# Graph network layer: 49 edge groups for 50, dense units inside stage A, source indices loaded first, and gathers paced one by one

## The reference

```python
def _L0_gnn_ref(x, edge_index, W1, b1, W2, b2):
    x_col = x[col]
    feat = jnp.concatenate([x_col, x[row] - x_col], axis=-1)
    h = jax.nn.relu(feat @ W1 + b1)
    messages = h @ W2 + b2
    out = jax.ops.segment_max(messages, col, num_segments=x.shape[0])
    return jnp.where(jnp.isneginf(out), jnp.zeros_like(out), out)
...
def _L1_gnn_ref(x, edge_index, W1, b1, W2, b2, Wres, bres):
    agg = jax.ops.segment_sum(x[src], dst, num_segments=x.shape[0])
    h = x + agg
    h = jnp.maximum(h @ W1 + b1, 0.0) @ W2 + b2
    return x @ Wres + bres + h
...
x = _layernorm(x + _L0_gnn_ref(x, edge_index, ...), axis=-1)
x = _layernorm(x + _L1_gnn_ref(x, edge_index, ...), axis=-1)
```

## Time and profile before

| what | value |
|---|---|
| median of 3 timed executions | 1454.56 us (1453.96 to 1475.86) |
| the profiled execution: its own time | 1442.36 us |
| its span, from first to last instruction | 1440.5 us |
| PE busy over the span | 1176.8 us (82%) |
| DVE, ACT, POOL busy | 1085.9, 818.3, 833.3 us |
| mean granted clock of PE | 0.957 of full speed |
| moved by DMA | 236.11 MB, 164 GB/s on the mean |

### The profile page before, as it was taken

How to read it: one execution, slowest core, us unless ns; L and a number is a source line. 1 busy time by engine, 2 the same in 40 slices (tenths; PEclk the granted TensorE clock), 3 DMA queues, 4 the chain that set the end, 5 groups by cost and what they waited for, 6 DMA issues and landing times. The chain is left out here.

```text
span 1440.5 us, 32925 instructions
## 1 busy us (share of the span) xinstructions
PE 1176.8 (82%) x7573; PEld 862.2 (60%) x7573; DVE 1085.9 (75%) x5525; ACT 818.3 (57%) x2320; POOL 833.3 (58%) x812
## 2 busy tenths in 40 slices
PE   3899999972277777777669998999899999999992
PEld 1667777651133334334357877887776777777771
DVE  6698999862177777777748897897787888888881
ACT  1355555541155555555426665665657777777772
POOL 2666666666666666665066666666655555555513
PEclk9899999987599999999879999999999999999996
DMA  3666666643256655556445565655655555556541
GB/s 96 179 193 195 204 199 196 194 130 94 53 175 175 171 176 168 169 172 156 122 123 177 173 194 160 193 182 165 177 177 152 175 180 184 182 188 187 180 142 50
DMA packets 162414, 236.11 MB, mean 164 GB/s; under 512 B 27296, under 2 KB 70526, under 8 KB 162369
## 3 DMA queue, kind: packets, MB, share of 16 engines
q1 hardware_dynamic: 135184, 195.53, 42.8%
q0 software_dynamic: 25600, 39.60, 11.3%
q10 hardware_dynamic: 1584, 0.53, 0.1%
HBM read 131.05 MB, written 90.91 MB: 154 GB/s over the span
## 5 line engine op out<-in xcount | busy, mean ns | idle before, releaser
L576 POOL DMA_INDIRECT out<-edge_rows,idx x200 | 201.7, 1008 | 190.7 <-issue 127.7
L1221 PE MATMUL psY<-wcr,xT 128*128 128x128 f32 x1568 | 305.3, 276 | 0.0
L1220 PE MATMUL psY<-wc,hT 128*128 128x128 f32 x1568 | 304.8, 276 | 0.5 <-issue 0.5
L569 POOL DMA_INDIRECT edge_rows<-x1e_table,idx x200 | 206.1, 1031 | 151.2 <-issue 96.9
L569 POOL DMA_INDIRECT edge_rows<-in_x,idx x200 | 214.0, 1070 | 134.4 <-issue 64.8
L569 POOL DMA_INDIRECT xd_rows<-in_x,idx x200 | 209.2, 1046 | 120.6 <-issue 63.9
L1220 PEld LDWEIGHTS psY<-wc,hT 128*128 128x128 f32 x1568 | 256.2, 194 | 7.3 <-issue 0.8
L1072 ACT ACTIVATE o_rows<-psY,rs_b 128x128 f32<-128x128 f32 x784 | 223.6, 368 | 56.0 <-issue 40.3
L1221 PEld LDWEIGHTS psY<-wcr,xT 128*128 128x128 f32 x1568 | 240.0, 193 | 0.0
L1231 PE MATMUL psH<-xT,wc 128*128 128x512 f32 x392 | 212.9, 625 | 16.7 <-issue 9.7
L1052 ACT ACTIVATE sd_a<-mv_a,eps_col 128x4 f32<-128x4 f32 x196 | 58.4, 298 | 274.4 <-issue 150.5
(11 more groups left out here) (131 smaller groups left out, 2132.2 us busy)
## 6 DMA issues: line engine op xcount, KB each, us to landing
x_in<-in_x SPq DMA_DIRECT2D x196, 256.0 KB
out<-o_rows SPq DMA_DIRECT2D x196, 256.0 KB
xs_rows<-edge_rows SPq DMA_DIRECT2D x100, 256.0 KB
xs_rows<-src_dram SPq DMA_DIRECT2D x50, 256.0 KB
mask<-mask_dram SPq DMA_DIRECT2D x100, 128.0 KB
x1e_table<-shared SPq DMA_DIRECT2D x50, 256.0 KB
x1eT_spill<-x1eT SPq DMA_DIRECT2D x50, 256.0 KB
x1eT<-x1eT_spill SPq DMA_DIRECT2D x50, 256.0 KB
```

The source lines that it names most:

```text
L569: nc.gpsimd.indirect_dma_start(to, None, table, bass.IndirectOffsetOnAxis(idx[:, what, t:t + 1], 0), bounds_check=rows - 1, oob_is_err=err ...
L576: nc.gpsimd.indirect_dma_start(table, bass.IndirectOffsetOnAxis(idx[:, SCAT, t:t + 1], 0), frm, None, bounds_check=N - 1, oob_is_err=False ...
L1220: t_.matmul(to[:, cut(t)], h[:, cut(t)], wc2[:, :], start=False, stop=False, skip_group_check=True)
L1221: last = t_.matmul(to[:, cut(t)], xt[:, cut(t)], wcr[:, :], start=False, stop=t == TILES - 1, skip_group_check=True)
```

## The change

- GROUPS becomes 49 (the number of groups that hold an edge), with one quad that holds a single group at the end.
- Stage A is walked in octets of eight steps, and ahead of every even step stands one dense unit: six octets take bodies 14 to 19. Stage B has bodies 20 to 31, and stage C begins with body 32 and keeps 17 of its 23 bodies.
- The source indices are loaded ahead of x, on a semaphore of their own, cast and transposed at once (SRC_IDX_STEP, step 2 of DVE's setup), and POOL begins its source gathers after that step.
- POOL's source groups 38 to 48 are gathered one by one behind destination groups 4, 8, 12, ... 44.
- `pace` and `issued_pair` give way to `one_behind`: every transfer signals `s_issued`, and POOL issues one when all but the latest have signalled.
- The counter of a scatter's group is loaded ahead of the last transfer of the group before.

```diff
-    GROUPS = 2 * -(-E // (2 * ROWS))
...
+    GROUPS = -(-E // ROWS)
...
+    OCTETS = GROUPS // (2 * SLOTS)
+    FIRST_A = 1 + QUADS
+    FIRST_B = FIRST_A + OCTETS
     FIRST_C = FIRST_B + QUADS - 1
+    SRC_FIRST = GROUPS - 11
...
-            def quad_a(j):
-                for r in range(SLOTS):
-                    step_a(j, r)
+            def octet_a(i, b):
+                for r in range(2 * SLOTS):
+                    j = i * 2 + r // SLOTS
+                    if r % 2 == 0:
+                        dense(b, r // 2)
+                    step_a(j, r % SLOTS)
...
+            sp.wait_ge(s_iz, 1)
+            load_indices(0, src, s_is)
             for k in range(3):
                 load(0, k)
...
-            pool.wait_ge(s_dv, IDX_STEP)
+            pool.wait_ge(s_dv, SRC_IDX_STEP)
...
-            def pace(kw):
+            def one_behind():
+
+                wait(pool, s_issued, issued[0] - 1)
                 issued[0] += 1
-                if issued[0] % 2 == 0:
-                    kw["engine_sem"] = s_issued
-
-            def issued_pair():
-                if issued[0] % 2 == 0:
-                    pool.wait_ge(s_issued, issued[0] // 2)
...
-            for g in range(GROUPS):
+            for g in range(SRC_FIRST):
                 gather_src(g)
                 if g == GROUPS // 2:
+                    pool.wait_ge(s_dv, IDX_STEP)
                     for d in range(SLOTS):
                         gather_dst(d)
+            late = SRC_FIRST
             for g in range(SLOTS, GROUPS):
                 gather_dst(g)
+                if g % 4 == 0 and late < GROUPS:
+                    gather_src(late)
+                    late += 1
...
+            def stores_needed(g):
+                earlier = pool.value_load(stores_16[0:1, g:g + 1], min_val=0, max_val=16 * LAST)
+                return pool.snap(earlier + 16)
...
                 for t in range(TILES):
+                    if t == TILES - 1 and g + 1 < WHOLE:
+                        count = stores_needed(g + 1)
                     scatter(out, edge_rows[:, cut(g * TILES + t)], g * TILES + t, final[r])
...
+            dve.wait_ge(s_is, 16 * 3)
+            link(v.tensor_copy(idx_f[:, 0, :, :], idx_in[:, 0, :, :]))
             norm1_stats(0, 0)
             norm1_ready(0, 0)
             norm1_var(0, 0)
+            dve.wait_ge(s_pe, 1)
+            link(v.tensor_copy(idx[:, 0, :], psE[0][:, 0:2 * P]))
```

More of the change, by code:

```diff
@@ L50, in gnn_program @@
     assert UNITS == BODIES * SLOTS and N % 32 == 0
-    GROUPS = 2 * -(-E // (2 * ROWS))
-    PAIRS = GROUPS // 2
+    GROUPS = -(-E // ROWS)
+    OF_PARITY = [len(range(q, GROUPS, 2)) for q in range(2)]
     ETILES = GROUPS * TILES
@@ L325, in walk @@
             quad_s(0, 1)
-            with eng.Fori(1, QUADS - 1) as j:
+            with eng.Fori(1, QUADS - 2) as j:
                 quad_s(j, j + 1)
-            quad_s(QUADS - 1, QUADS)
+            for j in (QUADS - 2, QUADS - 1):
+                quad_s(j, j + 1)
             lead_a()
[L330 to L334, removed]
+            octet_a(0, FIRST_A)
+            with eng.Fori(1, OCTETS - 1) as i:
+                octet_a(i, i + FIRST_A)
+            octet_a(OCTETS - 1, OCTETS - 1 + FIRST_A)
+            for r in range(SLOTS):
+                step_a(QUADS - 1, r)
             lead_b()
             quad_b(0, FIRST_B)
-            with eng.Fori(1, QUADS - 1) as j:
+            with eng.Fori(1, QUADS - 2) as j:
                 quad_b(j, j + FIRST_B)
+            quad_b(QUADS - 2, QUADS - 2 + FIRST_B)
             quad_b(QUADS - 1, None)
@@ L496, in step_b, with load_indices @@
                 feed_b(j, r + 1)
+            HALF = P * P
+            def load_indices(n, a, done):
+                sp.dma_start(idx_in[:, n, 0, :], a[0:HALF].rearrange("(j p) -> j p", p=P)).then_inc(done, 16)
+                sp.dma_start(idx_in[0:FULL - P, n, 1, :],
+                             a[HALF:FULL * P].rearrange("(j p) -> j p", p=P)).then_inc(done, 16)
+                sp.dma_start(idx_in[FULL - P:FULL - P + 1, n, 1, 0:REST],
+                             a[FULL * P:E].rearrange("(j p) -> j p", j=1)).then_inc(done, 16)
+            sp.wait_ge(s_iz, 1)
+            load_indices(0, src, s_is)
             for k in range(3):
                 load(0, k)
[L501 to L508, removed]
+            sp.wait_ge(s_iz, 2)
+            for n in (1, 2):
+                load_indices(n, dst, s_i)
             sp.dma_start(idx_in[:, 3, 0, :], dst[1:HALF + 1].rearrange("(j p) -> j p", p=P)).then_inc(s_i, 16)
@@ L539, in _ @@
         def _(pool):
-            nc.gpsimd.memset(idx_in[:, 0:2, :, :], 0)
+            nc.gpsimd.memset(idx_in[:, 0, :, :], 0).then_inc(s_iz, 1)
+            nc.gpsimd.memset(ident[:, :], 0.0)
+            nc.gpsimd.memset(center[:, :], -1.0 / P).then_inc(s_c2, 1)
+            nc.gpsimd.memset(idx_in[:, 1, :, :], 0)
             nc.gpsimd.memset(idx_in[:, 2, :, :], BIG)
             nc.gpsimd.memset(idx_in[:, 3:5, :, :], -1).then_inc(s_iz, 1)
-            nc.gpsimd.memset(ident[:, :], 0.0)
-            nc.gpsimd.memset(center[:, :], -1.0 / P).then_inc(s_c2, 1)
             pool.wait_ge(s_c2, 1)
@@ L948, in _ @@
             norm1_var(0, 0)
+            dve.wait_ge(s_pe, 1)
+            link(v.tensor_copy(idx[:, 0, :], psE[0][:, 0:2 * P]))
+            assert step[0] == SRC_IDX_STEP
             norm1_stats(0, 1)
@@ L1191, in _ @@
             pe.wait_ge(s_c, 1)
+            pe.wait_ge(s_dv, 1)
+            for h in range(2):
+                last = t_.transpose(psE[0][:, cut(h)], idx_f[:, 0, h, :], ident[:, :])
+            last.then_inc(s_pe, 1)
             pe.wait_ge(s_w, 16 * 11)
-            pe.wait_ge(s_dv, 1)
+            pe.wait_ge(s_dv, SRC_IDX_STEP + 1)
             t_.matmul(psE[2][:, 0:P], center[:, :], raw[:, W1R, :], start=True, stop=True)
@@ L1201, in _ @@
             pe.wait_ge(s_dv, SCAT_STEP)
-            for n in range(3):
+            for n in range(2):
                 for h in range(2):
-                    at = 2 * n + h
-                    last = t_.transpose(psE[at // 4][:, cut(at % 4)], idx_f[:, n, h, :], ident[:, :])
+                    last = t_.transpose(psE[1][:, cut(2 * n + h)], idx_f[:, 1 + n, h, :], ident[:, :])
             last.then_inc(s_pe, 1)
```

44 lines of the change are left out of this document (20 added, 24 removed).

## The result

| what | us |
|---|---|
| the changed kernel, median of 4 (1877.88 to 1888.19) | 1881.37 |
| the kernel before beside it, median of 4 (1453.96 to 1475.86) | 1460.53 |
| ratio, with its 95% interval | 1.2907 [1.2817, 1.2997] |
| span of its profiled execution, granted clock | 1880.2, 0.835 |

The forecast was 1371 us. The changed kernel took 29% longer than the kernel before, against 5.7% less.

What follows compares the result with a forecast made beforehand. No engine was full throughout: PE bound search, B and tail, a ring stage A. Terms -84 +14 -6.6 -4 -1.5 -1 -0.5 = -83.6 us gave span about 1357, time 1359, scaled by 1.0085 to 1371 us; range 1330 to 1420 us.

Steps and rivals of the forecast that it cites:

- Pacing: POOL's transfers: signalling each and waiting for all but the latest, starts come 1.31 us apart (bounds 1.31 and 1.57).
- Rival four: Stage A: POOL becomes the bound if dense work on DVE slows its gathers; 1495 us, chance 0.04.
- the 24 ns: What dense work costs a POOL gather: means 1070 ns mostly beside it, 1046 ns mostly without it.
- rival two: POOL's pace stays 1.57 us a transfer, so its last scatters end late: 39 us on top, 1410 us; chance 0.14.
- Does the stall go?: Start of stage A: the 51.5 us stall on late destination rows goes, as POOL's gathers end at 232 or 276 us.
- They enter stage A: One dense unit ahead of every even step: 16.9 us a pair, 24 pairs 406 us, +14 us with the stall gone.
- 84 off, 72 on: 24 dense units leave stage C, 84 us off at 3.49 us each, and add 72 us of work to stage A.
- the ring: Stage A's step: DVE, ACT and PE wait on each other in turn; even step about 10.0 us, odd 6.9.
- Tail: End of kernel: four scatters after the last store instead of eight, last starting 3.9 us on, not 10.6; -6.6 us.
- the slack: POOL's margin at the end: its chain ends at 1284 us, the last store lands at 1343; 59 us.
- slower: Outcome outside the 2% that can't be told from no change, on the slow side: chance 0.04.

Runs made afterwards that it cites:

- g_after: The changed kernel with no further edit, in a set where the kernel before took 1414.57 us: 1345.95 us, ratio 0.9511.
- h_no_dense_in_a: The changed kernel without dense units in stage A (bodies back in stage C), new pacing kept; kernel before 1414.5 us: 1316.56 us, ratio 0.9311.
- h_pairs: The changed kernel with the kernel before's pauses by pairs put back, all else kept; kernel before 1414.5 us: 1409.95 us, ratio 0.997.

## Why the prediction was wrong, step by step

**The step that failed is "Pacing".** Its claim on POOL held in part: the pause is gone and the gap is 0.30 us, but on the first kind starts are about 1.3 us apart in stage B and 1.50 in the search. It failed in what it left out. I priced the pause of 0.81 us on POOL alone, between bounds of 1.31 and 1.57 us a transfer, and never asked what it did for the other engines. On the second kind it is what lets them run: 29 to 33% of the time hang on it. Rival four was near in form (dense work and POOL's issuing hold each other up) but had the direction wrong for the second kind: it let DVE slow POOL, and here POOL slows all the others. On the first kind its direction shows in one stage. POOL of g_after in the search:

```profile
150.94 1.01 POOL L580 DMA_INDIRECT edge_rows<-in_x,idx  x1 [0.30 <-DMA edge_rows<-in_x,idx]
152.25 1.06 POOL L580 DMA_INDIRECT edge_rows<-in_x,idx  x1 [0.31 <-DMA edge_rows<-in_x,idx]
153.62 1.56 POOL L580 DMA_INDIRECT edge_rows<-in_x,idx  x1 [0.30 <-DMA edge_rows<-in_x,idx]
```

And POOL's busy time over 170 us, with the number of transfers, first of g_after, then of the changed kernel on the second kind:

```profile
60.00:230.00 170.00, 134.31 (x113) 1.00 0.74 217
```

```profile
60.00:230.00 170.00, 121.84 (x122) 0.51 0.22 59
```

Where PE and DVE run the search, a transfer takes 1.19 us on the mean (35 of the 113 over 1.3 us) and starts are 1.50 us apart; in the same stage with the others mostly standing still, 1.00 us and 1.39. So the 24 ns, read from a kernel with pauses, were too small, and 1.31 us was too short for the search; PE didn't have to wait for these gathers. Dense work alone isn't what lengthens them: in stage B, with PE at 98%, a transfer takes 1.02 us (the third of the windows below, 244.86 us for 241). What in the search does it is not shown, nor whether it has to do with the starving. Nothing in the rows of before could give the size, as in them no third transfer ever stands right behind two others. That was in the text, as an argument for rival two. It should have been the argument for a case on the slower side.

The Trainium skill, page "SBUF — State Buffer", section "Who interferes with whom", says that DMA never contends with a compute engine, and that only a port pair shared by DVE and GpSimd does. The 16 to 20% of PE in these runs are no proof against it, since the path is not known, but PE, which by that section shares no port with GpSimd, stood still as much as DVE. Whoever reads the rule as "gathers can't slow PE" is wrong by nearly a factor of five here (95% against 20%, one kernel on the two kinds).

**The rest can be judged on the first kind,** where the forecast of 0.9426 (1371/1454.56) met 0.9511. The windows of g_after: search, stage A, stage B, stage C.

```profile
28.00:285.00 257.00, 245.48 (x2006) 189.57 (x2034) 237.89 (x1239) 150.30 (x429) 181.57 (x155) 0.99 0.69 206
288.00:729.00 441.00, 328.22 (x1555) 201.45 (x1576) 308.50 (x1381) 243.66 (x615) 231.36 (x224) 0.96 0.53 156
755.00:1076.00 321.00, 314.64 (x2159) 261.92 (x2184) 281.82 (x1411) 210.77 (x657) 244.86 (x241) 0.99 0.61 190
1100.00:1318.00 218.00, 214.85 (x1449) 171.04 (x1465) 189.62 (x1190) 170.45 (x508) 125.64 (x119) 1.00 0.56 181
```

*Does the stall go?* Right. PE starts on xd_rows at 288.5 us and runs to the last step without a gap of tens of us.

*They enter stage A.* Too small. From 288.5 to 729.0 us are 24 pairs, 18.35 us each, inside the bounds of 13.5 to 18.9, but 1.45 above the 16.9 taken: 35 us in all. The same stage without them, in h_no_dense_in_a:

```profile
285.00:615.00 330.00, 237.69 (x1049) 131.76 (x1048) 242.45 (x945) 182.18 (x429) 230.69 (x224) 1.00 0.62 172
```

The steps there start over 329.5 us, 48 of them, 6.86 us each (forecast 6.9). So a unit in stage A costs (440.5 - 329.5)/24 = 4.63 us. Its price in stage C follows from all that lies behind stage A, where h_no_dense_in_a gathers first from the table at 633.69 us and g_after at 745.97:

```profile
633.69 1.00 POOL L577 DMA_INDIRECT edge_rows<-x1e_table,idx  x1 [39.41 <-DMA x1e_table<-shared]
```

To the ends of the spans, 1314.4 and 1343.9 us, are 680.7 and 597.9 us: 82.8 us for 24 units, 3.45 us each (forecast 3.49). To move them is a loss of 24 x 1.18 = 28 us, and 29.4 us were measured (1345.95 - 1316.56, in two sets whose kernel before agrees within 0.1 us). The forecast held it for a gain of 12 us: 84 off, 72 on. That sign was wrong, and the rest of the change carried it.

What the ring missed is seen in one even step, on DVE, PE and SP's queue of g_after:

```profile
652.84 0.75 DVE L874 SCALAR_TENSOR_TENSOR shared<-shared,bias_cols,xdT 128x512 f32<-128x512 f32 x1
...
657.78 0.49 DVE L682 BATCH_NORM_STATS2 bn_a<-x_in 128x6 f32<-128x128 f32 x2 [2.18 <-DMA x_in<-in_x]
...
662.11 0.20 DVE L841 RECIPROCAL rs_e<-sd_e 128x8 f32<-128x8 f32 x1 [1.15 <-ACT sd_e L1075]
...
664.27 0.75 DVE L874 SCALAR_TENSOR_TENSOR shared<-shared,bias_cols,xdT 128x512 f32<-128x512 f32 x1
666.52 0.89 DVE L663 BATCH_NORM_STATS2 bn_z<-psE 128x6 f32<-128x128 f32 x4 [1.50 <-PE psE L1237]
...
671.80 0.75 DVE L874 SCALAR_TENSOR_TENSOR shared<-shared,bias_cols,xdT 128x512 f32<-128x512 f32 x1
```

```profile
660.14 0.63 PE L1237 MATMUL psE<-ident,xd_rows 128*128 128x128 f32 x4 [1.67 <-ACT x1eT L1160]
...
662.66 1.91 PE L1342 MATMUL psE<-xdT,wd 128*128 128x512 f32 x2
```

```profile
653.02 0.35 SPq L437 DMA_DIRECT2D mask<-mask_dram  x1
653.58 0.35 SPq L377 DMA_DIRECT2D x_in<-in_x  x1
```

SP issues the load of the unit's x at 653.58 us, right behind the load of the mask, which waits until the scan has let go of its slot. The dense load itself waits for nothing there: it stands in an in-order queue behind an instruction that does. DVE wants that tile at 655.6 and gets it 2.18 us later (such waits sum to 26.1 us over 13 steps from 400 to 700 us). ACT, the copy of x1eT and PE's transposes at 660.14 follow late, and PE's next products run at a granted clock of 0.54 (662.5 to 666 us), 1.91 us for the two that take 1.13 at 290.69 us. Residual to residual the even step takes 11.4 us (forecast 10.0) and the odd one 7.5 (6.9), as it too begins with a wait for PE, 1.50 us. I asked of DVE, ACT and PE what is queued behind what, and not of SP. That this queue causes the loss is read from rows; no kernel with the load ahead of the mask was run.

*Tail.* Right, in rows of g_after's POOL:

```profile
745.97 1.00 POOL L580 DMA_INDIRECT edge_rows<-x1e_table,idx  x1 [42.65 <-DMA x1e_table<-shared]
...
1264.69 0.98 POOL L585 DMA_INDIRECT out<-edge_rows,idx  x1 [11.63 <-issue]
...
1292.20 0.98 POOL L585 DMA_INDIRECT out<-edge_rows,idx  x1 [22.66 <-issue]
...
1318.48 0.98 POOL L585 DMA_INDIRECT out<-edge_rows,idx  x1 [21.44 <-issue]
...
1329.94 0.98 POOL L585 DMA_INDIRECT out<-edge_rows,idx  x1 [6.62 <-DMA out<-o_rows]
...
1333.80 0.98 POOL L585 DMA_INDIRECT out<-edge_rows,idx  x1 [0.30 <-issue]
```

Four scatters from 1329.94 to 1333.80 us: 3.86 us (forecast 3.9). POOL's waits in the scatters sum to 11.63 + 22.66 + 21.44 + 6.62 = 62.3 us, the slack that was put at 59. Stage B's first gather came at 745.97, not 732: the pairs take 35 us more, and stage A begins some 21 us earlier than in the kernel before (first transposes at 288.1 us against 308.93), which was of the other kind. That the sum came out near is partly luck.

*Rival two*, the pace stays at 1.57, was worked out as 3% faster with POOL 37 us late. Forced by h_pairs it is 0.3% faster with POOL over 60 us late: right in kind, too small in size. The about 2 us of fixed cost, most of it the receipt, that the Trainium skill gives (page "DMA: Bandwidth & Descriptors", section "Anatomy of one DMA — SWDGE (gpsimd) path") don't touch this signal: with a wait for the signal ahead of each transfer the gap is 0.81 us.

*Range and chances.* The bound 1330 to 1420 us would have held on the first kind, by ratio 1383 us, with the dense units' wrong sign inside it. In the set that counted nothing of it held, and "slower" had 0.04.

## What to carry to other kernels

A pause on an engine that isn't the bottleneck may be there for the others: before it is taken away, look for a stretch of the trace that shows the resource without it, and if there is none, price the case in which it protects something. Gaps with "issue" on every engine at once, one instruction each few us, and little DMA traffic were here interference and not a missing buffer. Measure such a change in several sets: the new pacing alone gained 3% in four of them and lost 33% in a fifth. Dense work that is put beside a latency-bound ring has its loads in the same in-order queue as the ring's: issue them ahead of the one that waits. The safest version of those run is the pauses by pairs without dense units in stage A: by ratio 2.9% faster than before on the kind where the changed kernel is 29% slower, though whether by 2% is unclear. It wasn't run on the first kind, where the changed kernel without those units, but with the new pacing, gives 6.9%.

## What the hardware showed that was not expected

- Indirect transfers issued back to back, one always queued behind the running one, bring PE, DVE, ACT and SP's transfers nearly to a halt in some sets: PE 16 to 20% busy, one matmul each 2.80 us at times, DMA at 33 to 65 GB/s. In others the same program runs PE at 95% and 204 GB/s. A gap of 0.81 us after every second transfer, with a signal for every second, removes most of it (PE 90 to 95%), one after every fourth only a part (63%).
- POOL's transfers issued back to back take 1.19 us on the mean and up to 1.56 in the search of g_after, 1.00 us in the same stage where the others mostly stand still, and 1.02 us in stage B of g_after beside a PE at 98%.
- What passes between POOL and the others is not shown, nor why sets differ, nor whether the chip decides it. The kernel before is 1.5 to 3.3% slower on the kind that starves; its PE is at 95% in the search, where h_pairs has 100% on the first kind.
- PE's granted clock went to 0.52 in these stretches, 0.98 in the next: a consequence, since a matmul of 0.37 us in 2.80 isn't explained by a clock at half.
